# A mixture-of-experts slot loop: GpSimd's scatter moved behind the next slot's power, with four output buffers

## The chip, the cores and the metric

The kernel runs on one core of one Trainium2 chip. A core has five engines that run side by side: TensorE (PE: matmuls and transposes), VectorE (DVE), ScalarE (ACT), GpSimd (POOL) and SyncE (SP), and 16 DMA engines that carry the transfers. The engines wait for each other with semaphores only; each runs its own instructions in order. The metric is the time of one execution on the device, in microseconds, as the median over runs.

## The reference, cut to what matters

Tokens x (2048 rows of 512) first pass a quantized graph layer with an adjacency matrix (2048 x 2048), then a top-2 mixture of 16 experts. The change lies in the second part:

```python
x = x + gnn(layernorm(x), adj, ...)
xn = layernorm(x)
logits = xn @ Wr + br
topk_w, topk_idx = top_k(softmax(logits), 2)        # weights scaled to a sum of 1
h = einsum('nc,ech->neh', xn, W1) + b1
h = gelu(layernorm(h, g1, be1))
y = einsum('neh,eho->neo', h, W2) + b2
out = x + sum over the two chosen experts of topk_w * y
```

All of it is float32. The kernel computes an expert only for the tokens that chose it.

## The kernel before

**Stages.** From 0 to about 220 us the graph layer and the routing run. After them comes the stage of experts, written as slots. A slot is 128 tokens of one expert. The 4096 choices make 39 slots; one of expert 0 is computed early, and slots 0 to 37 form the loop. The last slot of an expert is padded, its spare rows go to rows behind the output. The number of slots is found at run time: `rest` is 17 here, and pair j of the loop is slots 2j and 2j+1, for j from 1 to rest; slots 36 and 37 end it. The experts after the first ones take 1 to 4 slots each; in this input new experts start at slots 5, 7, 10, 13, 16, 18, 19, 21, 23, 24, 28, 30, 32 and 36, and the first three slots (0, 1, 2) alternate between experts 1 and 0, so each counts as a start as well.

**What a slot does.** Rows of normed tokens are gathered from `xn_rows` into `xg` by an indirect DMA of GpSimd (line 747). TensorE transposes them (line 1756), ScalarE and VectorE make a high and a low part (lines 967 and 1392), and TensorE multiplies three times by the weights' high and low parts (lines 1846, 1850, 1854). VectorE takes the statistics of the result (lines 1396 to 1399), GpSimd makes the reciprocal root with a power (line 758, the `power` of this document, output `h_rs`), and VectorE norms (line 1483, `h_hat`). TensorE transposes that (line 1870), ScalarE applies gelu and makes the high part (lines 1021, 1026), VectorE the low one (line 1488), and TensorE multiplies by the second weights (lines 1846 to 1854 again). ScalarE scales the product with the gate into `y_sb` (line 1000), and GpSimd adds these rows to `out` with an accumulating indirect DMA (line 774, the scatter).

**What sets the order.** Everything is ordered by hand, in software pipelining. TensorE's slot s is: transpose h_hat of s (line 1870), transpose the rows of s+3 (line 1756), second layer of s-1, first layer of s+2. GpSimd's iteration s (line 796) is: power of slot s+1, `fetch(s)`, which waits for the gate value of slot s+3 and then gathers the rows of slot s+5, and `give(s - 1)`, which scatters slot s-1. GpSimd runs in order, so while the scatter waits, nothing behind it starts.

**What a scatter waits for** (lines 778 to 783). Two scatters in flight must not add to the same row. Within an expert all rows differ, so only two conditions remain: the scatter of slot s-2 has landed, and, where slot s starts an expert (`start` is 1), that of slot s-1 too. Landings are counted on two semaphores, `scattered[0]` for even and `scattered[1]` for odd slots, 16 for each DMA. Each semaphore begins with 16 from a DMA that fills the spare rows (line 647). The third wait, `y_ok`, is for ScalarE's product. ScalarE in turn waits, ahead of line 1000, until the scatter that used the same half of `y_sb` (slot n-2) has landed.

**Weights.** SyncE loads the weights of an expert's two layers (1 MB each, lines 602 to 609) when those of the expert two before have been split. ScalarE and VectorE split them into high and low parts at each start of an expert (lines 1004 to 1008 and 1460).

**Memory.** `y_sb` holds 2 buffers of 128 x 512, in the space of the support matrix `sup`, which the expert stage no longer needs. Behind `sup` lies the space of the adjacency steps, also free by then.

Of the kernel before, what the change touches and what calls it, by code (L numbers as in the profile page):

```python
# [30 lines left out]
P = 128  # L31
# [154 lines left out]
def gnn_moe_program(nc, x, adj_steps, gnn_w, scalars, wr, br, w1, b1, g1, be1, w2, b2, consts, xn_rows, bias_dram, out):  # L186
    with ExitStack() as ctx:
# [117 lines left out]
        y_sb = place("y_sb", [P, 2, D], F32)  # L305
# [4 lines left out]
        assert where[0] <= end_sup  # L310

# [303 lines left out]
        def _(pool):  # L615
# [31 lines left out]
            for h in range(2):  # L647
                pool.dma_start(out[N + h * P // 2:N + (h + 1) * P // 2, :], k_sb[h * P // 2:(h + 1) * P // 2, 0:D]
                               ).then_inc(scattered[h], 16)
# [122 lines left out]
            def add_rows(at, par):  # L772
                pool.sem_inc(pool_turn, 1)
                pool.indirect_dma_start(  # L774
                    out, bass.IndirectOffsetOnAxis(ap=at, axis=0),
                    y_sb[:, par, :], None, compute_op=ALU.add).then_inc(scattered[par], 16)

            def give(s, start):

                pool.wait_ge(scattered[s % 2], s // 2 * 16 + 16)  # L780
                pool.wait_ge(scattered[1 - s % 2], start * 16 + (s + 1) // 2 * 16)
                pool.wait_ge(y_ok, s + 3)
                add_rows(scat_i[:, s:s + 1], s % 2)
# [9 lines left out]
            give(0, 1)  # L793
            def pool_pair(j):
                earlier, word = load_begins(pool, j - 1), load_begins(pool, j)
                for s in (2 * j, 2 * j + 1):
                    slot_rstd(s + 1, (s + 1) % 2)
                    fetch(s)
                    give(s - 1, (word & 1) if s % 2 else (earlier >> 1))
# [9 lines left out]
            def give_last(back, done, starts):  # L809

                par = (3 - back) % 2
                pool.wait_ge(scattered[par], done)
                pool.wait_ge(scattered[1 - par], starts)
                pool.wait_ge(y_ok, rest * 2 + (4 + back))
                add_rows(idx_s[:, back:back + 1], par)
# [10 lines left out]
        def _(act):  # L826
# [169 lines left out]
            def gated(n, par, landed):  # L996

                act.wait_ge(mm2, n + 1)
                act.wait_ge(scattered[par], landed)
                act.activation(y_sb[:, par, :], y_ps(par), ACT.Copy, scale=gate[:, bass.ds(n + 1, 1)]).then_inc(y_ok, 1)  # L1000
# [33 lines left out]
            def slot(s, par, word, landed, last=False):  # L1034
# [7 lines left out]
                gated(s - 1, 1 - par, landed)  # L1042
# [14 lines left out]
            slot(1, 1, word, 16)  # L1057
            def act_pair(j):
                word = load_plan(act, j)
                for par in range(2):  # L1060
                    slot(j * 2 + par, par, word, j * 16 + 16 * par)
# [9 lines left out]
            for par in range(2):  # L1071
                slot(rest * 2 + (2 + par), par, word, rest * 16 + (16 + 16 * par), last=True)
            gated(rest * 2 + 3, 1, rest * 16 + 32)
# [893 lines left out]
```

## Time and profile before

| | us |
|---|---|
| median of 3 runs | 496.46 |
| lowest and highest run | 492.79, 497.95 |
| profiled execution, its own time | 496.7 |
| its span (first to last instruction) | 494.9 |
| TensorE busy | 456.1 (92%) |
| VectorE busy | 349.9 (71%) |
| ScalarE busy | 306.5 (62%) |
| GpSimd busy | 231.2 (47%) |
| GpSimd, scatter of line 774 (35 of the 38; the last 3 take their indices from `idx_s`) | 64.2 busy, 35.5 idle ahead of it |
| GpSimd, gather of line 747, 40 | 47.3 busy, 57.5 idle ahead of it |
| GpSimd, power of line 758, 38 | 25.1 busy, 31.4 idle ahead of it |
| granted TensorE clock, mean | 0.985 |

Busy time is that in which an engine works on an instruction; for an indirect DMA it is the time in which GpSimd writes its descriptors, and the transfer goes on after it. An idle time stands with what ended it. A row of a timeline has the start, the duration, the engine, the line, the operation, what is written and read, how many instructions were merged, and in brackets the idle time of the engine ahead of it with its releaser. The chain that ended last is followed back from the last instruction, at each step to what released it.

### The profile page before, as it was taken

To read this page: it belongs to the slowest core of one execution; us is meant where nothing else is said; L and a number is where in the kernel's file an instruction comes from. 1 tells how busy PE (TensorE), PEld (TensorE's weight loads), DVE (VectorE), ACT (ScalarE), POOL (GpSimd) and SP (SyncE) were. 2 spreads that over 40 slices of the span, in tenths; PEclk is the share of its full clock that TensorE was granted. 3 is DMA by queue.
4 is the path that set the end of the run, shared out by engine and by line. 5 is a ranking of instruction groups with operands and counts; after the bars stand their busy time and mean duration, and the time that the engine had idled before them with its cause. 6 is when DMAs were issued, how large, how long until landed. Compare 5 with 4: busy or idle time off the path is not lost.

```text
span 494.9 us, 10329 instructions
## 1 busy us (share of the span) xinstructions
PE 456.1 (92%) x2260; PEld 376.2 (76%) x2261; DVE 349.9 (71%) x735; ACT 306.5 (62%) x511; POOL 231.2 (47%) x267
## 2 busy tenths in 40 slices
PE   0799999989999999989899999999899989999990
PEld 0578888877888888867677888888787768888870
DVE  5898863777788877875657786667877777677720
ACT  1667462474544334445787878788888777897550
POOL 4373330332155637553446555554645455356532
PEclk9999999999999999898999999999999999999996
DMA  8621224884655643249849787958699879674543
GB/s 304 262 84 45 86 64 171 299 303 171 221 162 172 214 134 134 84 115 315 260 114 272 186 239 210 263 124 233 210 250 296 248 188 323 149 192 87 86 67 42
DMA packets 33533, 91.30 MB, mean 184 GB/s; under 512 B 6161, under 2 KB 6305, under 8 KB 32993
## 3 DMA queue, kind: packets, MB, share of 16 engines
q1 hardware_dynamic: 19664, 60.60, 36.9%
q0 software_dynamic: 9232, 21.98, 20.9%
q10 hardware_dynamic: 4608, 8.39, 4.6%
q8 instruction: 11, 0.18, 0.1%
q14 instruction: 18, 0.14, 0.1%
HBM read 71.89 MB, written 19.07 MB: 184 GB/s over the span
## 4 chain that ended last, share of the span: by engine, by line
PE 68%; DMA 11%; DVE 6%; issue 5%; ACT 3%; POOL 2%; DVEq 1%; POOLq 1%; ACTq 0%; SPq 0%
PE ps L1595 15%; PE ps L1846 10%; PE ps L1854 9%; PE ps L1850 9%; PE ps L1567 6%; PE ps L1579 6%; DMA out<-y_sb,scat_i 5%; PE ps L1756 3%; PE ps L1870 2%; DMA xg<-xn_rows,tok_i 2%; PE ps L1635 2%; PE ps L1555 1%; DMA xn_rows<-xn 1%; PE ps L1699 1%; DMA gw_raw<-in_gnn_w 1%
## 5 line engine op out<-in xcount | busy, mean ns | idle before, releaser
L774 POOL DMA_INDIRECT out<-y_sb,scat_i x35 | 64.2, 1835 | 35.5 <-DMA out<-y_sb,scat_i 21.9
L1460 DVE TENSOR_TENSOR w_split<-w_raw,w_split x56 | 67.1, 1220 | 12.1 <-issue 9.7
L747 POOL DMA_INDIRECT xg<-xn_rows,tok_i x40 | 47.3, 1183 | 57.5 <-ACT gate L972 49.0
L1021 ACT ACTIVATE g_sb<-ps,be_sb,g_sb 128x128 f32<-128x128 f32 x152 | 57.0, 456 | 16.0 <-PE ps L1870 15.8
L832 ACT ACTIVATE adj_hi<-adj_raw,small 128x1024 fp32r<-128x1024 f32 x32 | 36.8, 1150 | 41.4 <-PE ps L1595 34.5
L1007 ACT ACTIVATE w_split<-w_raw x28 | 53.0, 1912 | 7.8 <-DMA w_raw<-in_w 6.6
L1153 DVE SCALAR_TENSOR_TENSOR adj_lo<-adj_raw,small,adj_hi 128x1024 fp32r<-128x1024 f32 x32 | 40.8, 1275 | 20.6 <-ACT adj_hi L832 20.5
L1595 PE MATMUL ps<-sup,adj_lo 128*128 128x512 f32 x192 | 49.2, 398 | 0.0
L1595 PE MATMUL ps<-sup,adj_hi 128*128 128x512 f32 x192 | 49.2, 398 | 0.0
L1483 DVE TENSOR_SCALAR h_hat<-ps,h_mv,h_rs 128x512 f32<-128x512 f32 x38 | 30.7, 808 | 23.1 <-POOL h_rs L758 23.1
L658 POOL TENSOR_SCALAR rstd<-mv 128x1 f32<-128x1 f32 x15 | 13.7, 914 | 67.6 <-DVE mv L1193 67.5
L1846 PE MATMUL ps<-w_split,gt_hi 128*128 x152 | 44.5, 415 | 0.6 <-ACT gt_hi L1026 0.6
L1854 PE MATMUL ps<-w_split,gt_hi 128*128 x152 | 41.1, 392 | 1.5 <-DVE w_split L1460 1.5
L1488 DVE TENSOR_TENSOR gt_lo<-g_sb,gt_hi 128x512 fp32r<-128x512 f32 x38 | 26.2, 688 | 22.6 <-issue 18.2
L1850 PE MATMUL ps<-w_split,gt_lo 128*128 x152 | 41.0, 392 | 0.1
L1846 PE MATMUL ps<-w_split,xt_hi 128*128 x148 | 40.9, 399 | 0.0
L1595 PEld LDWEIGHTS ps<-sup,adj_lo 128*128 128x128 f32 x192 | 34.9, 188 | 6.9
L1850 PE MATMUL ps<-w_split,xt_lo 128*128 x148 | 40.2, 394 | 0.0
L1595 PEld LDWEIGHTS ps<-sup,adj_hi 128*128 128x128 f32 x192 | 35.0, 188 | 6.8
L758 POOL TENSOR_TENSOR h_rs<-h_rs,k_sb 128x1 f32<-128x1 f32 x38 | 25.1, 662 | 31.4 <-DVE h_rs L1399 31.4
L1854 PE MATMUL ps<-w_split,xt_hi 128*128 x148 | 39.7, 390 | 0.0
L1000 ACT ACTIVATE y_sb<-ps,gate 128x512 f32<-128x512 f32 x38 | 26.1, 687 | 16.6 <-PE ps L1854 15.9
(216 smaller groups left out, 958.0 us busy)
## 6 DMA issues: line engine op xcount, KB each, us to landing
w_raw<-in_w SPq DMA_DIRECT2D x64, 512.0 KB, 6.5
adj_raw<-in_adj_steps SPq DMA_DIRECT2D x32, 512.0 KB, 3.5
out<-x_sb ACTq DMA_DIRECT2D x16, 256.0 KB, 2.9
xn_rows<-xn ACTq DMA_DIRECT2D x16, 256.0 KB, 3.0
bias_rows<-in_b SPq DMA_DIRECT2D x16, 256.0 KB, 3.3
x_sb<-in_x SPq DMA_DIRECT2D x3, 1024.0 KB, 12.3
gw_raw<-in_gnn_w SPq DMA_DIRECT2D x1, 1024.0 KB, 4.9
x_sb<-in_x SPq DMA_DIRECT2D x2, 512.0 KB, 6.8
```

What stands on the lines that cost most here:

```text
L747: return pool.indirect_dma_start(to, None, xn_rows, bass.IndirectOffsetOnAxis(ap=tok_i[:, s:s + 1], axis=0)).then_inc(landed[s % 2], 16)
L774: pool.indirect_dma_start(out, bass.IndirectOffsetOnAxis(ap=at, axis=0), y_sb[:, par, :], None, compute_op=ALU.add).then_inc(scattered[par ...
L832: act.activation(adj_hi[:, par, :], adj_raw[:, par, :], ACT.Copy, scale=small[:, 0:1]).then_inc(adj_hi_ok, 1)
L1007: act.activation(w_parts(n, 0, e + 1), w_raw[:, n, :, :].rearrange("p a n -> p (a n)")[:, at], ACT.Copy).then_inc(split_hi[n], 1)
L1021: ins = act.activation(g_sb[:, par, c * P:(c + 1) * P], ht_ps(par)[:, c * P:(c + 1) * P], ACT.Gelu, scale=g1_sb[:, bass.ds(e * C + c, 1)], ...
L1153: dve.scalar_tensor_tensor(adj_lo[:, par, :], adj_raw[:, par, :], small[:, 0:1], adj_hi[:, par, :].bitcast(F32), ALU.mult, ALU.subtract).t ...
L1460: return dve.tensor_tensor(w_parts(n, 1, e + 1, 2 * h, 2), w_raw[:, n, :, :].rearrange("p a n -> p (a n)")[:, at], w_parts(n, 0, e + 1, 2 ...
L1483: dve.tensor_scalar(h_hat[:, par, :], h_ps(par), h_mv[:, par, 0:1], h_rs[:, par, 0:1], ALU.subtract, ALU.mult).then_inc(h_hat_ok, 1)
L1595: ins = pe.matmul(acc_bank(t), part[:, n % 2, k * P:(k + 1) * P], sup[:, first_k + k, :], start=first_k + k == 0 and not half, stop=first_ ...
L1846: pe.matmul(dst, act_hi[:, par, c * P:(c + 1) * P], w_part(n, 0, e, c), start=False, stop=False, skip_group_check=n == 1)
L1850: pe.matmul(dst, act_lo[:, par, c * P:(c + 1) * P], w_part(n, 0, e, c), start=False, stop=False, skip_group_check=n == 1)
L1854: ins = pe.matmul(dst, act_hi[:, par, c * P:(c + 1) * P], w_part(n, 1, e, c), start=False, stop=c == C - 1, skip_group_check=n == 1)
```

## The change

The order within GpSimd's iteration s becomes: power of slot s+1, scatter of slot s-2, gather of slot s+5. Each slot's scatter so goes out about one slot later than before. Slot 0's scatter moves from ahead of the loop into the first pair. For the last pair (`rest == j`, decided at run time) the scatter of slot 2j is issued behind the pair, so the three last scatters find everything before them issued.

The product lives longer, so it gets four buffers in turn (`y_ring`, by slot modulo 4), and the last three slots have buffers of their own (`y_last`). Both lie in the space of the adjacency steps. ScalarE waits for the landing of the scatter of slot n-4 instead of n-2, and for none in the last three slots. The spare rows are filled by four DMAs of 32 rows instead of two of 64, so each semaphore begins with 32; all counts of landings rise by 16, with ScalarE's in the loop left as they were, which is what moves its wait back by two slots. What each scatter itself waits for stays the same.

```diff
@@ -302,12 +302,16 @@
-        y_sb = place("y_sb", [P, 2, D], F32)
...
+        where[0] = end_sup
+        y_ring = place("y_ring", [P, 4, D], F32)
+        y_last = place("y_last", [P, 3, D], F32)
+        assert where[0] <= w_at
@@ -644,9 +648,9 @@
-            for h in range(2):
-                pool.dma_start(out[N + h * P // 2:N + (h + 1) * P // 2, :], k_sb[h * P // 2:(h + 1) * P // 2, 0:D]
-                               ).then_inc(scattered[h], 16)
+            for h in range(4):
+                pool.dma_start(out[N + h * P // 4:N + (h + 1) * P // 4, :], k_sb[h * P // 4:(h + 1) * P // 4, 0:D]
+                               ).then_inc(scattered[h % 2], 16)
@@ -769,18 +773,18 @@
             def give(s, start):
 
-                pool.wait_ge(scattered[s % 2], s // 2 * 16 + 16)
-                pool.wait_ge(scattered[1 - s % 2], start * 16 + (s + 1) // 2 * 16)
+                pool.wait_ge(scattered[s % 2], s // 2 * 16 + 32)
+                pool.wait_ge(scattered[1 - s % 2], start * 16 + ((s + 1) // 2 * 16 + 16))
                 pool.wait_ge(y_ok, s + 3)
-                add_rows(scat_i[:, s:s + 1], s % 2)
+                add_rows(scat_i[:, s:s + 1], y_ring[:, s % 4, :], s % 2)
@@ -790,13 +794,15 @@
             pool.wait_ge(e_scattered, 16)
-            give(0, 1)
             def pool_pair(j):
-                earlier, word = load_begins(pool, j - 1), load_begins(pool, j)
+                earlier = load_begins(pool, j - 1)
                 for s in (2 * j, 2 * j + 1):
                     slot_rstd(s + 1, (s + 1) % 2)
+                    give(s - 2, (earlier >> (s % 2)) & 1 if j > 1 or s % 2 else 1)
                     fetch(s)
-                    give(s - 1, (word & 1) if s % 2 else (earlier >> 1))
+                if j >= SURE:
+                    with pool.If(rest == j):
+                        give(2 * j, load_begins(pool, j) & 1)
@@ -809,10 +815,10 @@
-                pool.wait_ge(scattered[par], done)
-                pool.wait_ge(scattered[1 - par], starts)
+                pool.wait_ge(scattered[par], done + 16)
+                pool.wait_ge(scattered[1 - par], starts + 16)
                 pool.wait_ge(y_ok, rest * 2 + (4 + back))
-                add_rows(idx_s[:, back:back + 1], par)
+                add_rows(idx_s[:, back:back + 1], y_last[:, back, :], par)
@@ -993,11 +999,12 @@
-            def gated(n, par, landed):
+            def gated(n, par, rows, landed=None):
 
                 act.wait_ge(mm2, n + 1)
-                act.wait_ge(scattered[par], landed)
-                act.activation(y_sb[:, par, :], y_ps(par), ACT.Copy, scale=gate[:, bass.ds(n + 1, 1)]).then_inc(y_ok, 1)
+                if landed is not None:
+                    act.wait_ge(scattered[par], landed)
+                act.activation(rows, y_ps(par), ACT.Copy, scale=gate[:, bass.ds(n + 1, 1)]).then_inc(y_ok, 1)
@@ -1054,11 +1061,12 @@
             def act_pair(j):
                 word = load_plan(act, j)
                 for par in range(2):
-                    slot(j * 2 + par, par, word, j * 16 + 16 * par)
+                    slot(j * 2 + par, par, word, y_ring.rearrange("p a d -> p (a d)")[:, bass.ds(((j * 2 + (par + 3)) & 3) * D, D)],
+                         j * 16 + 16 * par)
```

GpSimd's instructions of one pair in the middle of the loop, before. `TENSOR_TENSOR h_rs` is the power, `DMA xg` the gather, `DMA out` the scatter, `TENSOR_LOAD begins` reads the flags of expert starts into a register; of the two such loads that a pair begins with, the second is the first row here.

```order
L491 TENSOR_LOAD begins
L491 ISA x2
L758 TENSOR_TENSOR h_rs<-h_rs,k_sb 128x1
L747 DMA xg<-xn_rows,tok_i 128x528
L781 ISA
L774 DMA out<-y_sb,scat_i 2176x512
L758 TENSOR_TENSOR h_rs<-h_rs,k_sb 128x1
L747 DMA xg<-xn_rows,tok_i 128x528
L781 REGISTER_ALU
L781 ISA
L774 DMA out<-y_sb,scat_i 2176x512
```

The same pair after the change:

```order
L495 TENSOR_LOAD begins
L495 ISA x2
L762 TENSOR_TENSOR h_rs<-h_rs,k_sb 128x1
L785 REGISTER_ALU
L785 ISA
L778 DMA out<-y_ring,scat_i 2176x512
L751 DMA xg<-xn_rows,tok_i 128x528
L762 TENSOR_TENSOR h_rs<-h_rs,k_sb 128x1
L785 REGISTER_ALU x2
L785 ISA
L778 DMA out<-y_ring,scat_i 2176x512
L751 DMA xg<-xn_rows,tok_i 128x528
```

In both halves of the pair the scatter stood behind the gather, so just ahead of the next half's power, and now it stands between the power and the gather. One load of the flags is gone, and a compare (line 804) with the scatter of slot 2j behind it is new; that part is skipped in all pairs but the last.

Behind the stage's entry the scatter of slot 0 was the last instruction ahead of the first pair. The rows of GpSimd around the first pair's beginning, before:

```order
L758 TENSOR_TENSOR h_rs<-h_rs,k_sb 128x1
L747 DMA xg<-xn_rows,tok_i 128x528
L774 DMA out<-y_sb,scat_i 2176x512
L491 TENSOR_LOAD begins
L491 ISA x2
L491 TENSOR_LOAD begins
L491 ISA x2
L758 TENSOR_TENSOR h_rs<-h_rs,k_sb 128x1
L747 DMA xg<-xn_rows,tok_i 128x528
L781 ISA
L774 DMA out<-y_sb,scat_i 2176x512
L758 TENSOR_TENSOR h_rs<-h_rs,k_sb 128x1
```

and after:

```order
L762 TENSOR_TENSOR h_rs<-h_rs,k_sb 128x1
L751 DMA xg<-xn_rows,tok_i 128x528
L495 TENSOR_LOAD begins
L495 ISA x2
L762 TENSOR_TENSOR h_rs<-h_rs,k_sb 128x1
L778 DMA out<-y_ring,scat_i 2176x512
L751 DMA xg<-xn_rows,tok_i 128x528
L762 TENSOR_TENSOR h_rs<-h_rs,k_sb 128x1
L785 REGISTER_ALU x2
L785 ISA
L778 DMA out<-y_ring,scat_i 2176x512
L751 DMA xg<-xn_rows,tok_i 128x528
```

The first power of the pair (slot 3) had the scatter of slot 0 ahead of it and has nothing of the kind now, and slot 0's and slot 1's scatters follow the powers of slots 3 and 4.

## Rows read from the trace of the kernel before

**Rows 1.** The page, section 4: shares of the chain that ended last.

```profile
PE 68%; DMA 11%; DVE 6%; issue 5%; ACT 3%; POOL 2%; DVEq 1%; POOLq 1%; ACTq 0%; SPq 0%
```

**Rows 2.** The chain that ended last: start us, us, what.

```profile
363.57 8.91 DMA out<-y_sb,scat_i
```

**Rows 3.** Windows: us, PE, PEld, DVE, ACT, POOL busy (x), PEclk, DMA share, GB/s.

```profile
241.40:268.00 26.60, 25.90 (x129) 21.12 (x128) 16.86 (x30) 19.81 (x38) 14.55 (x13) 1.00 0.69 173
...
341.00:407.00 66.00, 61.16 (x301) 49.48 (x300) 51.22 (x76) 53.50 (x93) 32.86 (x28) 1.00 0.81 234
407.00:473.00 66.00, 66.00 (x333) 55.37 (x334) 45.79 (x76) 49.78 (x95) 36.51 (x32) 1.00 0.67 166
```

**Rows 4.** Timeline of TensorE: start us, us, engine line op, [idle before <-releaser].

```profile
255.06 0.66 PE L1870 MATMUL ps<-k_sb,h_hat 128*128 128x128 f32 x4 [0.26 <-DVE h_hat L1483]
...
262.31 0.66 PE L1870 MATMUL ps<-k_sb,h_hat 128*128 128x128 f32 x4 [0.44 <-DVE h_hat L1483]
...
301.89 0.60 PE L1870 MATMUL ps<-k_sb,h_hat 128*128 128x128 f32 x4
...
308.47 0.60 PE L1870 MATMUL ps<-k_sb,h_hat 128*128 128x128 f32 x4
...
349.41 0.65 PE L1870 MATMUL ps<-k_sb,h_hat 128*128 128x128 f32 x4 [1.30 <-issue]
...
377.26 0.65 PE L1870 MATMUL ps<-k_sb,h_hat 128*128 128x128 f32 x4 [1.15 <-DVE h_hat L1483]
...
384.35 0.60 PE L1756 MATMUL ps<-k_sb,xg 128*128 128x128 f32 x4
...
402.44 1.20 PE L1854 MATMUL ps<-w_split,gt_hi 128*128 x4 [1.47 <-DVE w_split L1460]
```

**Rows 5.** Timeline of GpSimd, an undisturbed slot.

```profile
303.39 0.57 POOL L758 TENSOR_TENSOR h_rs<-h_rs,k_sb 128x1 f32<-128x1 f32 x1 [0.94 <-DVE h_rs L1399]
305.69 1.01 POOL L747 DMA_INDIRECT xg<-xn_rows,tok_i  x1 [1.73 <-ACT gate L972]
307.40 2.13 POOL L774 DMA_INDIRECT out<-y_sb,scat_i  x1 [0.70 <-issue]
```

**Rows 6.** Waits, 240 to 496 us: us in total, times, longest us.

```profile
POOL out L774 <- DMA out<-y_sb,scat_i: 21.9, 8, 5.8
```

**Rows 7.** Timeline of GpSimd, the stage's beginning.

```profile
251.96 1.60 POOL L774 DMA_INDIRECT out<-y_sb,scat_i  x1 [5.75 <-DMA out<-y_sb,scat_i]
253.01 1.14 POOL L758 TENSOR_TENSOR h_rs<-h_rs,k_sb 128x1 f32<-128x1 f32 x1
```

**Rows 8.** Timeline of VectorE around late powers.

```profile
249.28 0.15 DVE L1399 TENSOR_SCALAR h_rs<-h_mv 128x1 f32<-128x1 f32 x1
254.19 0.81 DVE L1483 TENSOR_SCALAR h_hat<-ps,h_mv,h_rs 128x512 f32<-128x512 f32 x1 [4.76 <-POOL h_rs L758]
...
374.12 0.15 DVE L1399 TENSOR_SCALAR h_rs<-h_mv 128x1 f32<-128x1 f32 x1
...
396.44 0.81 DVE L1483 TENSOR_SCALAR h_hat<-ps,h_mv,h_rs 128x512 f32<-128x512 f32 x1 [1.69 <-POOL h_rs L758]
```

**Rows 9.** Timeline of GpSimd, slots 21 to 24.

```profile
373.33 1.58 POOL L774 DMA_INDIRECT out<-y_sb,scat_i  x1 [2.47 <-DMA out<-y_sb,scat_i]
374.39 1.12 POOL L758 TENSOR_TENSOR h_rs<-h_rs,k_sb 128x1 f32<-128x1 f32 x1
375.70 1.01 POOL L747 DMA_INDIRECT xg<-xn_rows,tok_i  x1 [0.19 <-issue]
...
395.29 1.12 POOL L758 TENSOR_TENSOR h_rs<-h_rs,k_sb 128x1 f32<-128x1 f32 x1
```

**Rows 10.** Timeline of ScalarE, a split that waits for weights.

```profile
387.00 1.92 ACT L1007 ACTIVATE w_split<-w_raw  x1 [3.89 <-DMA w_raw<-in_w]
```

**Rows 11.** Line 774, the scatter: from issue to landing.

```profile
DMA to landing us min/median/max: 4.8/8.5/9.7
```

**Rows 12.** Line 747, the gather: from issue to landing.

```profile
DMA to landing us min/median/max: 3.3/4.4/8.0
```

More of the change, by code:

```diff
@@ L770, in fetch, with add_rows @@
                 gather(s + 5)
-            def add_rows(at, par):
+            def add_rows(at, rows, par):
                 pool.sem_inc(pool_turn, 1)
@@ L775, in add_rows @@
                     out, bass.IndirectOffsetOnAxis(ap=at, axis=0),
-                    y_sb[:, par, :], None, compute_op=ALU.add).then_inc(scattered[par], 16)
+                    rows, None, compute_op=ALU.add).then_inc(scattered[par], 16)
             def give(s, start):
-                pool.wait_ge(scattered[s % 2], s // 2 * 16 + 16)
-                pool.wait_ge(scattered[1 - s % 2], start * 16 + (s + 1) // 2 * 16)
+                pool.wait_ge(scattered[s % 2], s // 2 * 16 + 32)
+                pool.wait_ge(scattered[1 - s % 2], start * 16 + ((s + 1) // 2 * 16 + 16))
                 pool.wait_ge(y_ok, s + 3)
-                add_rows(scat_i[:, s:s + 1], s % 2)
+                add_rows(scat_i[:, s:s + 1], y_ring[:, s % 4, :], s % 2)
             early_scatter()
@@ L1032, in slot_seed, with slot @@
                 act.activation(y_ps(par), bias_rows2[:, bass.ds((e & 3) * D, D)], ACT.Copy).then_inc(y_seeded, 1)
-            def slot(s, par, word, landed, last=False):
+            def slot(s, par, word, rows, landed=None, last=False):
                 e_s, e_a = expert_in(word, par), expert_in(word, par + 2)
@@ L1041, in slot @@
                     slot_gate(s + 3, 1 - par, expert_in(word, par + 3))
-                gated(s - 1, 1 - par, landed)
+                gated(s - 1, 1 - par, rows, landed)
                 if not last:
@@ L1056, in _ @@
             split_next(1, expert_in(word, 0), starts_in(word, 0))
-            slot(1, 1, word, 16)
+            slot(1, 1, word, y_ring[:, 0, :])
             def act_pair(j):
@@ L1071, in _ @@
             for par in range(2):
-                slot(rest * 2 + (2 + par), par, word, rest * 16 + (16 + 16 * par), last=True)
-            gated(rest * 2 + 3, 1, rest * 16 + 32)
+                slot(rest * 2 + (2 + par), par, word, y_last[:, par, :], last=True)
+            gated(rest * 2 + 3, 1, y_last[:, 2, :])
             for par in range(2):
@@ L1076, in _ @@
             for i in range(2):
-                act.wait_ge(scattered[i], rest * 16 + 48)
+                act.wait_ge(scattered[i], rest * 16 + 64)
             act.sem_inc(all_landed, 1)
```

## The prediction

> **What bounds the kernel now.** I read the chain that ended last first, then the stages in windows, then TensorE's timeline slot by slot, then GpSimd's. The chain is 68% TensorE, but 11% of the span on it is DMA [rows 1], and the scatter of line 774 is its largest part. One piece of the chain is the 8.91 us in which slot 18's scatter, issued at 363.57, lands [rows 2]. The windows show where TensorE is not full. From 241.40 to 268.00 it is busy 25.90 of 26.60 us, from 341 to 407 it is busy 61.16 of 66.00, and from 407 to 473 all 66.00 [rows 3]. The granted clock is 1.00 in all three. So the expert stage runs at TensorE's own pace except in two places, with 0.70 and 4.84 us of idle time.
>
> The pace is one slot per 6.58 us: slot 11's hidden transpose starts at 301.89 and slot 12's at 308.47 [rows 4]. I write S for the time at which a slot's hidden transpose starts. A slot can gain only where its distance from the one before exceeds 6.58. These are slot 4 (7.05, from slot 3 at 248.01), slot 5 (7.25), slot 18 (349.41, 8.04 after slot 17), slot 22 (377.26, 7.94 after slot 21), slot 24 (7.43) and slot 26 (8.87, with the wait at 402.44 inside it); all other excesses are 0.1 or less. The sum of all excesses from slot 2 to slot 36 is 7.7 us, the ceiling of the whole change. Slot 18's part, 1.46 us, is "issue", a wait for nothing in the profile, which I leave out. That leaves 6.2.
>
> **What happens on GpSimd.** In an undisturbed slot (S = 301.89) the power starts at S+1.50, the gather at S+3.80 and the scatter at S+5.51, for 2.13 us [rows 5]. The scatter is the last thing before the next power, which comes at S+8.08. If the scatter waits for its predecessor to land, the power behind it is late. Line 774 waits for a landing 8 times, 21.9 us in all, at most 5.8 [rows 6]. At slot 4 this reaches TensorE. The scatter at 251.96 waited 5.75 us, the power behind it ended at 254.15 [rows 7], though VectorE had asked for it at 249.28+0.15. VectorE waited 4.76 us with h_hat [rows 8], and TensorE started its transpose at 255.06 [rows 4].
>
> **The change, part by part.**
>
> (1) The order in a slot becomes power, scatter of slot s-2, gather. The product that the scatter takes has long been ready (it was made in the slot before, at about S-2), so the scatter waits for no ScalarE and can start at about S+1.50+0.57+0.3 = S+2.4. The gather follows: before, GpSimd stood idle there for 1.73 us, waiting for the gate value [rows 5]. The scatter takes 1.6 to 2.6 us, so the gather starts at S+4.2 to S+5.3 instead of S+3.8.
>
> Gain at slots 4 and 5: both excesses (0.47 and 0.67) come from the late power, the second because VectorE is then late with the splits and statistics of the next slot. With the power in front, it starts at about S(3)+1.5 = 249.5 and not 253.01. I take both in full and the 0.1 behind them: -1.2.
>
> Gain at slot 22: the power starts at 374.39 and takes 1.12 us instead of 0.57, since the scatter issued at 373.33 still runs [rows 9]. VectorE's request was ready at 374.27 [rows 8]. Without the scatter it would end at about 375.0 instead of 375.5: 0.5 us at most. The rest of this excess is older than GpSimd's part. ScalarE and VectorE were themselves late with weight splits, and the next split waits 3.89 us for a weight transfer that lands at 387.0 [rows 10]; the gain at 22 is likely absorbed there. I take 0.2, with 0 and 0.5 as bounds, and nothing for slot 24.
>
> Gain at slot 26: the power at 395.29 takes 1.12 us behind a scatter [rows 9], and VectorE waits 1.69 us for it instead of the 0.6 or so of a power alone [rows 8]. From there the chain runs through VectorE's sequencer and a split to the matmul at 402.44. I take 0.8, with 0 and 2.3 as bounds.
>
> (2) The ring of four. ScalarE waits for the landing of slot n-4 instead of n-2. This wait was seen once, 0.7 us, with ScalarE idle right behind it for a weight transfer: nothing. The ring is also what makes (1) legal, as the scatter now reads the product one slot later. Its register address costs ScalarE two sequencer instructions a slot, in slots where it has idle time.
>
> (3) Two more small DMAs at the start, about 1 us of GpSimd each by the gather's row [rows 5]. They lie in the support phase and feed nothing but a semaphore and, behind them, casts first used in the adjacency windows: nothing. Were that cover gone, 2 us.
>
> (4) The end. The scatter of slot 2*rest still goes out one slot early, behind an If, and the last three keep their places and their waits; the buffers of their own remove waits of ScalarE that had already ended. Nothing. Two loads of "begins" per pair become one, and a compare is added: nothing.
>
> (5) What is pushed back is the gather, and this is the cost. The gather issued in slot s is used by the row transpose of slot s+2, 0.43 us behind its hidden transpose, so at S+13.6; it had 9.8 us. Gathers take 3.3 to 8.0 us, median 4.4 [rows 12]. The tightest one now is issued at 375.70, takes the 8.0 and lands at 383.7; the transpose starts at 384.35 [rows 4, 9]. It has 0.6 us to spare. In the changed kernel its scatter (slot 19, a start of an expert behind another) must first see slot 18 land, at about 374.3, if that one is issued at 365.4 and takes its 8.9 us again [rows 2]. Then the scatter goes at 375.3, the gather at 377.2, and it lands 1.5 us later than before, or 0.9 us too late for TensorE. In the other slots with an expert start the scatter waits 0 to 3 us and the gather lands 0.7 before to 0.7 behind its use. I take +0.9, with 0 and +7 as bounds (below).
>
> Something speaks for a higher price. The gather of 8.0 us was issued only 2.4 us behind a scatter [rows 9], the quiet gather at 305.69 nearly 5 us behind one, and the median gather takes 4.4. The Trainium skill (DMA: Bandwidth & Descriptors, Two DMAs through the same engine are not ordered) states that within one queue of an engine descriptors start in order. By that rule a gather right behind a scatter cannot land much ahead of it: in two or three more slots with weight transfers it would come in too late, and the sum would be about 2 us higher; without it the 0.9 stands. By it, the one row agrees, and it is part of what rival (A) below would look like.
>
> **Sum.** -1.2 - 0.2 - 0.8 + 0.9 = -1.3 us on the profiled execution's 496.7 us (its span of 494.9 and 1.8 around it): 495.4. That execution lies 0.2 above the median of the three runs, 496.46, so I name 495.2.
>
> **Rivals.**
>
> (A) The gather becomes the wait. A scatter that lands 8.5 us (median) to 9.7 us behind its issue [rows 11], one slot of 6.58 before, makes the next expert's first scatter wait 1.9 to 3.1 us, plus some 0.9 from landing to issue. The gather then starts as late as S+2.4+4.0+2.1+0.3 = S+8.8, and with a latency of 4.4 to 8.0 lands at S+13.2 to S+16.8, against S+13.6: up to 3.2 us late. This would show as TensorE waiting at line 1756 on the DMA of xg. With all 8 waits ending in a gather 0.9 us late, 7.2 us are lost and 2.2 gained: 501.7, or 501.5 against the median. With three such (2.7 lost) the result is 497.0, so from the third on the change loses. Against it: each stall of TensorE also gives the scatters time. It is the case of the other side. Chance 0.2, of which 0.1 over 1%.
>
> (B) The dense stretch clears. The chain runs from 355.0 to 373.3 through the landings of two scatters. If these, and not the weights, set VectorE's lateness, slots 22, 24 and 26 return their 1.36 + 0.85 + 2.29 = 4.5 us; with the 1.2 and no late gather that is 491.0, or 490.8 against the median. For it: the chain itself [rows 2]. Against it: the splits wait for weight transfers at 387.0 [rows 10], and VectorE's request at slot 22 was only 0.1 us ahead of the power. Chance 0.17.
>
> (C) Nothing moves. The weight transfers hold the dense stretch, the first cluster's 1.2 us is eaten by one late gather, and the change does not do what it says because the scatter still stands ahead of the next power and can run into it. GpSimd's room ahead of the next power grows from 0.4 us (scatter's end to S+8.08) to between 1.8 and 2.8 (gather's end at S+5.2 to S+6.3), so a longer wait still reaches the power. That gives 496.5. Chance 0.13.
>
> The forecast itself, 493.5 to 496.2, has 0.5.
>
> **From the cases to the numbers.** About 1% (5 us) is what a measurement of this kernel can tell from no change; its own three runs span 492.79 to 497.95. Faster by over 1% means under 491.5: most of (B), 0.13. Slower by over 1% means over 501.4: half of (A), 0.1. Same: 0.77. The range goes from 490.5, just beyond (B), to 499.5, which holds the milder half of (A), with 10% left out above and a few per cent below.
>
> **What would show it.** Right: powers of slots 4 and 5 at S+1.5 of the slot before; TensorE's busy time in 241 to 268 full; no power of over 0.6 us that starts inside a scatter; no wait of h_hat for the power above 0.7 us. Step (5): a wait at line 1756 for xg around slot 23, of under 2 us, and gather starts between S+4.2 and S+5.3 in slots without an expert start. Wrong: waits at line 1756 in four slots or more (A); slots 22 to 26 all 6.6 apart (B); a ScalarE wait for scattered, or the last three scatters later against TensorE's end.

## The result and the profile after

The change makes the kernel slower: median 497.28 us of 20 runs (494.42 to 500.36), against 493.67 us for the kernel before in the same session (20 runs, 491.14 to 497.95). The ratio is 1.0062, 95% interval 1.0041 to 1.0082. A second comparison gave 1.0086 (1.0058 to 1.0114). The forecast was 1.3 us faster, so it is wrong in sign, though the time lies in its range and within 1% of the kernel before. The forecast's base also moved: 496.46 us was the median of three runs, and the median of 20 is 2.8 us lower. Ratios leave out the executions of a kernel that were over 1.5% longer than its fastest, so they can differ from the quotient of two medians.

The profiled execution of after took 496.24 us, with a span of 494.4. That is no longer than the one of before, but before's began its slots late: slot 2's hidden transpose starts at 241.40 there and at 238.52 here. So the two are compared from slot 2's transpose to slot 36's, and from there to the end.

| us | before | before, 2nd profile | after | after, 2nd profile |
|---|---|---|---|---|
| slot 2 to slot 36 (34 slots; 223.7 at 6.58 each) | 231.4 | 231.2 | 233.1 | 232.7 |
| slot 36 to the end | 22.1 | 22.0 | 22.8 | 23.0 |
| TensorE's waits for gathered rows, slot 2 to 36 | none | 0.2 | 5.0 | 3.7 |

On average the slots cost 1.6 us more and the end 0.8. The medians differ by 3.6 and 3.5 us; about 1 us of it is in none of these four profiles.

The page of after, section 4, the chain that ended last by engine (before: [rows 1]); and from section 5 GpSimd's three groups: line, engine, operation, count, then busy us, mean ns, and idle us ahead with the main releaser.

```profile
PE 54%; DMA 15%; issue 12%; POOL 6%; DVE 5%; ACT 3%; ACTq 1%; POOLq 1%; SPq 0%; DVEq 0%
...
L778 POOL DMA_INDIRECT out<-y_ring,scat_i x35 | 65.1, 1860 | 24.0 <-DMA out<-y_ring,scat_i 12.7
...
L751 POOL DMA_INDIRECT xg<-xn_rows,tok_i x40 | 48.0, 1200 | 24.1 <-ACT gate L978 11.0
L762 POOL TENSOR_TENSOR h_rs<-h_rs,k_sb 128x1 f32<-128x1 f32 x38 | 22.1, 582 | 74.5 <-DVE h_rs L1407 74.3
```

The power is no longer held up: 582 ns mean, and its idle time ends with VectorE's statistics. The scatter's idle time fell from 35.5 to 24.0 us. But the gather's idle time fell too, from 57.5 to 24.1 us. Most of it had been a wait for the gate value, so it was reserve: the gather could not start earlier, but what stood ahead of it could take longer without moving it. The waits from slot 2 to slot 36 of after, in us in total, times, longest:

```profile
DVE h_hat L1491 <- POOL h_rs L762: 16.5, 23, 1.5
POOL out L778 <- DMA out<-y_ring,scat_i: 12.7, 12, 4.3
PEld ps L1764 <- DMA xg<-xn_rows,tok_i: 6.6, 7, 1.8
PE ps L1764 <- DMA xg<-xn_rows,tok_i: 5.0, 6, 1.5
```

The first two lines are what the change aims at: against [rows 6] the scatter's waits fell from 21.9 to 12.7 us, and VectorE's longest wait for a power from 4.76 [rows 8] to 1.5. One more wait, 2.8 us ahead of slot 1's scatter at 250.03, stands in the profile as one for ScalarE's product, but that product was written at 242.70; slot 0's scatter, which it needs, landed at 249.14. The last two lines are new. TensorE's timeline has four of the six:

```profile
259.69 0.66 PE L1764 MATMUL ps<-k_sb,xg 128*128 128x128 f32 x4 [0.80 <-DMA xg<-xn_rows,tok_i]
300.30 0.66 PE L1764 MATMUL ps<-k_sb,xg 128*128 128x128 f32 x4 [0.34 <-DMA xg<-xn_rows,tok_i]
341.43 0.66 PE L1764 MATMUL ps<-k_sb,xg 128*128 128x128 f32 x4 [0.98 <-DMA xg<-xn_rows,tok_i]
384.04 0.66 PE L1764 MATMUL ps<-k_sb,xg 128*128 128x128 f32 x4 [1.52 <-DMA xg<-xn_rows,tok_i]
```

The others are at 398.51 (0.94 us) and 412.48 (0.39 us). The rows waited for are those of slots 8, 14, 20, 26, 28 and 30 (TensorE is in slots 5, 11, 17, 23, 25 and 27). Each of these gathers stands behind the scatter of the first slot of an expert (slots 1, 7, 13, 19, 21, 23). One of them, slot 20's, on GpSimd's timeline of after:

```profile
329.51 0.57 POOL L762 TENSOR_TENSOR h_rs<-h_rs,k_sb 128x1 f32<-128x1 f32 x1 [4.27 <-DVE h_rs L1407]
330.53 2.33 POOL L778 DMA_INDIRECT out<-y_ring,scat_i  x1 [0.46 <-issue]
333.17 1.54 POOL L751 DMA_INDIRECT xg<-xn_rows,tok_i  x1 [0.30 <-issue]
```

and the same place in before, where the gather came straight behind the power:

```profile
331.26 0.57 POOL L758 TENSOR_TENSOR h_rs<-h_rs,k_sb 128x1 f32<-128x1 f32 x1 [1.49 <-DVE h_rs L1399]
332.02 1.99 POOL L747 DMA_INDIRECT xg<-xn_rows,tok_i  x1 [0.19 <-issue]
334.32 2.12 POOL L774 DMA_INDIRECT out<-y_sb,scat_i  x1 [0.31 <-issue]
```

Slot 15 starts at 326.60 in after and at 328.21 in before. The power comes 2.9 us behind that start in after (3.05 in before), not 1.5, because it waits for VectorE's statistics. No landing is waited for here. The gather starts at S+6.57, against S+3.81 in before, and its rows land 8.2 us later, at 341.38, just as TensorE begins at 341.43.

The line that times the gather from issue to landing in after (before: [rows 12]), then the scatter's (before: [rows 11]):

```profile
DMA to landing us min/median/max: 3.3/5.7/8.3
```

```profile
DMA to landing us min/median/max: 4.7/5.6/10.2
```

The gather's median rose from 4.4 to 5.7 us and the scatter's fell from 8.5 to 5.6. Both steps are too large: [rows 11] holds the landings of the even slots' scatters alone, since two records of the odd ones are missing in that profile. In the second profiles, which have all landings, the gather's median is 4.9 in before and 5.1 in after, and the scatter's 6.8 and 5.7.

### The profile page after: what moved, and what is told of

Same layout as the page of the kernel before. It is cut to its first block, busy times and chain, and to the rows that moved or that the text cites. A ratio compares the mean times of both kernels' runs of the same rounds, so it can differ in the third digit from the quotient of the medians.

```text
span 494.4 us, 10394 instructions
## 1 busy us (share of the span) xinstructions
PE 456.0 (92%) x2260; PEld 375.8 (76%) x2261; DVE 350.7 (71%) x735; ACT 306.0 (62%) x511; POOL 232.3 (47%) x269
## 4 chain that ended last, share of the span: by engine, by line
PE 54%; DMA 15%; issue 12%; POOL 6%; DVE 5%; ACT 3%; ACTq 1%; POOLq 1%; SPq 0%; DVEq 0%
PE ps L1603 15%; DMA xg<-xn_rows,tok_i 7%; PE ps L1575 6%; PE ps L1587 6%; PE ps L1854 6%; PE ps L1862 5%; PE ps L1858 5%; DMA out<-y_ring,scat_i 4%; POOL out L778 2%; POOL xg L751 2%; PE ps L1643 2%; PE ps L1764 2%; PE ps L1563 1%; DMA adj_raw<-in_adj_steps 1%; PE ps L1878 1%
## 5 line engine op out<-in xcount | busy, mean ns | idle before, releaser
L778 POOL DMA_INDIRECT out<-y_ring,scat_i x35 | 65.1, 1860 | 24.0 <-DMA out<-y_ring,scat_i 12.7
L751 POOL DMA_INDIRECT xg<-xn_rows,tok_i x40 | 48.0, 1200 | 24.1 <-ACT gate L978 11.0
L762 POOL TENSOR_TENSOR h_rs<-h_rs,k_sb 128x1 f32<-128x1 f32 x38 | 22.1, 582 | 74.5 <-DVE h_rs L1407 74.3
L1404 DVE BATCH_NORM_STATS2 h_stats<-ps 128x6 f32<-128x512 f32 x38 | 26.3, 693 | 15.6 <-PE ps L1862 15.4
```

What stands on the lines that cost most here:

```text
L751: return pool.indirect_dma_start(to, None, xn_rows, bass.IndirectOffsetOnAxis(ap=tok_i[:, s:s + 1], axis=0)).then_inc(landed[s % 2], 16)
L778: pool.indirect_dma_start(out, bass.IndirectOffsetOnAxis(ap=at, axis=0), rows, None, compute_op=ALU.add).then_inc(scattered[par], 16)
```

## The experiments

**Theory 1**: the order on GpSimd makes the loss, since the gather now stands behind power and scatter and comes too late in some slots; the ring costs nothing. **Rivals**: the loss is the ring's or its place in memory; or the late powers remain; or the slots' excesses belong to the weights and the waits for rows only show beside them. All ratios are against the kernel before on the same chip.

| run | median, us | ratio (95%) | slot 2 to 36 | to the end | waits for rows |
|---|---|---|---|---|---|
| ring_only | 493.32 | 1.0007 (0.9970 to 1.0044) | 232.0 | 22.2 | 0 |
| order_only | 497.01 | 1.0066 (1.0037 to 1.0095) | 234.6 | 22.7 | 5.0 |
| gather_first | 501.35 | 1.0143 (1.0094 to 1.0191) | 235.6 | 22.6 | 0 |
| no_scatter | 490.55 | 0.9914 (0.9881 to 0.9946) | 226.9 | 20.5 | 0 |
| pad_scatter | 488.19 | 0.9884 (0.9868 to 0.9901) | 226.3 | 20.5 | 0 |
| after_xg | 491.75 | 0.9942 (0.9906 to 0.9979) | 230.1 | 22.2 | 0 |
| after_xg_again | 491.65 | 0.9981 (0.9948 to 1.0015) | 229.7 | 22.0 | 0 |
| after_xg_third | 492.32 | 0.9971 (0.9949 to 0.9993) | 229.7 | 22.2 | 0 |
| before_xg | 493.28 | 0.9981 (0.9955 to 1.0007) | 229.4 | 21.9 | 0 |
| before_xg_again | 492.54 | 0.9983 (0.9945 to 1.0021) | 233.6 | 21.9 | 0 |

### The parts apart: ring alone, order alone

The ring, the last slots' own buffers and the four fills, with the old order of scatters (against after; the scatter behind the last pair goes too):

```diff
+            give(0, 1)
...
-                earlier = load_begins(pool, j - 1)
+                earlier, word = load_begins(pool, j - 1), load_begins(pool, j)
-                    give(s - 2, (earlier >> (s % 2)) & 1 if j > 1 or s % 2 else 1)
                     fetch(s)
...
+                    give(s - 1, (word & 1) if s % 2 else (earlier >> 1))
```

> The four buffers, the three of the last slots, the four fill DMAs and the counts, but GpSimd's old order: power, gather, scatter of slot s-1. Theory 1 (the loss is the gather that starts behind the scatter): ratio to before 0.998 to 1.001, TensorE waits for xg 0 times in the slots, and the late powers at slots 4, 5, 22 and 26 are there again. Rival (the loss lies in the other parts: register addresses on ScalarE, the fill DMAs): ratio 1.003 to 1.008.

Ratio 1.0007: these parts cost nothing that can be measured, as steps (2) and (3) of the prediction had it. The new order with two buffers for y (against after):

```diff
-        y_ring = place("y_ring", [P, 4, D], F32)
+        y_ring = place("y_ring", [P, 2, D], F32)
...
-                add_rows(scat_i[:, s:s + 1], y_ring[:, s % 4, :], s % 2)
+                add_rows(scat_i[:, s:s + 1], y_ring[:, s % 2, :], s % 2)
...
-                         j * 16 + 16 * par)
+                         j * 16 + (16 + 16 * par))
```

> The new order on GpSimd with y in two buffers instead of four (the last slots keep three of their own): ScalarE writes y of slot n when the scatter of slot n - 2 has landed. Theory 1 (the order alone makes the loss): that scatter is issued 2 to 5 us into slot n and y of slot n is written 4.3 us into the next slot, 6 to 9 us later, and scatters land 4.8 to 10.2 us after their start: ScalarE waits in a few slots, 1 to 5 us in all, and the time is that of after or up to 2 us more, ratio to before 1.004 to 1.012. Rival (the larger ring or its place in memory makes the loss): ratio 0.998 to 1.002, as with the ring alone.

Ratio 1.0066, the loss of after, so the loss is the order's. TensorE waits for rows here too, 5.0 us in six waits. ScalarE's waits were mis-sized: 19.4 us where 1 to 5 were expected.

```profile
ACT y_ring L1007 <- DMA out<-y_ring,scat_i: 19.4, 8, 3.7
```

Its slots took 1.5 us more than after's first profile, but its median is not above after's (497.01 against 497.28 and 497.77), so nothing shows that the two extra buffers earn anything. In after the same view puts 4.9 us of ScalarE's waits on landings, but each of those products was started 0.36 us behind the end of TensorE's last matmul for it, as in the slots with no such entry: they are waits for TensorE.

### The second profiles

> The kernel after once more, for a second profile. Theory 1: TensorE waits at least 2 us in all for gathered rows in the loop, in slots whose gather stands behind a scatter of an odd slot, ratio to before 1.003 to 1.009. Rival (the waits of the first profile were chance): under 1 us, ratio the same.

3.7 us of waits for rows, in slots 9, 17, 23, 25 and 29 (after's first profile: 5, 11, 17, 23, 25 and 27): the mechanism is there again, in partly other slots.

> The kernel before once more, for a second profile of the slot loop. Theory 1 (the first profiles told the truth on the loop): from slot 2's hidden transpose to slot 36's some 231 us (231.4 in the first profile; 233.1 and 232.7 in the two of after), at least one power held up by a scatter that waits for a landing, no wait of TensorE for gathered rows over 0.5 us, and 22.1 us from slot 36 to the end (22.8 and 23.0 in after). Rival (the loop's times differ by chance): 232.5 us or more, or waits for rows.

231.2 us, as expected. But the excesses are elsewhere. GpSimd's timeline in this second profile of before has the late power of [rows 7] again:

```profile
248.76 1.60 POOL L774 DMA_INDIRECT out<-y_sb,scat_i  x1 [4.71 <-DMA out<-y_sb,scat_i]
249.82 1.14 POOL L758 TENSOR_TENSOR h_rs<-h_rs,k_sb 128x1 f32<-128x1 f32 x1
```

A landing that was waited for 1 us less was enough: from slot 3's transpose to slot 6's it is 0.23 us over the pace, against 1.25 in the first profile. So the 1.2 us that the prediction put there is the size of one execution.

### The gather ahead of the scatter

Power, gather, scatter of slot s-2 (against after):

```diff
-                    give(s - 2, (earlier >> (s % 2)) & 1 if j > 1 or s % 2 else 1)
                     fetch(s)
+                    give(s - 2, (earlier >> (s % 2)) & 1 if j > 1 or s % 2 else 1)
```

> The changed kernel with two lines exchanged: power, gather, scatter of slot s-2. The scatter needs no wait for ScalarE's product, so it can start about 0.6 us sooner than in the kernel before, and the gather starts as before. Theory 1: no wait of TensorE for xg, powers less late than before, ratio to before 0.994 to 1.000. Rival (it is the scatter that comes one slot later, or the ring, that costs): ratio 1.003 to 1.008 like the changed kernel.

The waits for rows are gone, and the kernel is the slowest of all, where 0.994 to 1.000 was expected and the rival had 1.008 at most. GpSimd's timeline, and VectorE's at the same place:

```profile
275.95 1.02 POOL L751 DMA_INDIRECT xg<-xn_rows,tok_i  x1 [0.19 <-issue]
282.37 1.57 POOL L778 DMA_INDIRECT out<-y_ring,scat_i  x1 [5.40 <-DMA out<-y_ring,scat_i]
283.43 1.13 POOL L762 TENSOR_TENSOR h_rs<-h_rs,k_sb 128x1 f32<-128x1 f32 x1
```

```profile
279.77 0.15 DVE L1407 TENSOR_SCALAR h_rs<-h_mv 128x1 f32<-128x1 f32 x1
284.60 0.81 DVE L1491 TENSOR_SCALAR h_hat<-ps,h_mv,h_rs 128x512 f32<-128x512 f32 x1 [4.67 <-POOL h_rs L762]
```

The scatter stands last ahead of the next power again. It waits 5.40 us for its predecessor to land, and the power that VectorE asked for at 279.92 runs at 283.43; slots 8 and 9 then took 6.95 and 9.06 us, since VectorE was late with the next splits and statistics as well. This is the late power of before, [rows 7, 8], with longer waits (28.8 us in 7 waits for landings against 21.9 in 8). The one-slot delay of the scatter does not protect the power: each scatter still has only the one ahead of it to wait for, issued about a slot earlier. What protects the power is the place, and that place is paid for by the gather.

### Time on GpSimd, or the scatter's packets?

The scatters of slots 0 to 33 and ScalarE's waits for their buffers are left out, so the output lacks these slots; in the second run a fill of an unused buffer stands in the scatter's place:

```diff
-                    give(s - 2, (earlier >> (s % 2)) & 1 if j > 1 or s % 2 else 1)
+                    pool.wait_ge(y_ok, s + 1)
...
+                    pool.memset(pad_sb[:, :], 0.0).then_inc(pad_ok, 1)    # the second run only
                     fetch(s)
```

> The kernel after, without the scatters of slots 0 to 33 (they, their waits for landings and the multiplier engine's wait for their buffers are left out, so these slots' results are not added to the output; the scatters behind the loop stay). GpSimd then does power and gather and nothing between. Theory 1 (the gather, standing behind power and scatter, became late; the scatter costs nothing else): no wait of TensorE for gathered rows within the loop, no scatter in front of a power, so of the 9.4 us that the slots 2 to 36 take over 6.58 us each in the profile of after, the 5.0 us of waits for rows go, and what weights cost (slots 17, 23 to 26) stays: 3 to 7 us less than after, ratio to before 0.988 to 0.998. Rival (the slots' lateness is that of the weights and VectorE's splits, the rows' lateness only shows beside it): the waits for rows vanish but the slots stay at 8 to 10 us over, ratio 1.000 to 1.006.

> As the run without scatters, but GpSimd fills a buffer that nobody reads (128 x 2048, whose like took 1.81 us elsewhere in the kernel) where the scatter stood, behind the power and ahead of the gather: the time on GpSimd stays about that of the scatter (1.9 us mean), its packets and its waits for landings are gone. Theory 1a (the gather is late because it is issued late): TensorE still waits 2 to 5 us in all for rows in the slots where VectorE's splits hold the power back, the time is within 2 us of after's (ratio to before 1.001 to 1.008). Theory 1b (it is late because its packets stand behind the scatter's in one queue, or behind a scatter that waits for a landing): the gather's latencies in these slots fall from 7.4 to 8.3 us to 4 to 7 us, the waits are under 1 us in all, and the time is that of the run without scatters to 1 us.

Both lose the waits for rows. In the run with the fill the place of slot 20's gather reads (its slot 15 starts at 322.56, so the gather at S+5.55):

```profile
325.61 0.56 POOL L765 TENSOR_TENSOR h_rs<-h_rs,k_sb 128x1 f32<-128x1 f32 x1 [4.65 <-DVE h_rs L1416]
326.13 1.80 POOL L807 MEMSET pad_sb<- 128x2048 f32 x1
328.11 0.99 POOL L754 DMA_INDIRECT xg<-xn_rows,tok_i  x1 [0.17 <-issue]
...
DMA to landing us min/median/max: 3.3/4.0/7.1
```

The six gathers that were late, by their start behind S of the slot in which they are issued, and from start to landing, all in us:

| rows of slot | before | after | fill, no scatter |
|---|---|---|---|
| 8 | 6.3, 3.8 | 6.9, 7.6 | 4.0, 4.4 |
| 14 | 3.8, 6.8 | 6.4, 7.7 | 5.2, 4.0 |
| 20 | 3.8, 7.2 | 6.6, 8.2 | 5.6, 4.3 |
| 26 | 6.4, 8.0 | 8.9, 7.4 | 6.0, 7.0 |
| 28 | 8.4, 5.6 | 8.8, 7.7 | 6.5, 6.7 |
| 30 | 6.9, 7.7 | 7.2, 8.3 | 7.3, 5.9 |
| mean | 5.9, 6.5 | 7.5, 7.8 | 5.8, 5.4 |

From before to after they start 1.5 us later and take 1.3 us longer. With the fill they start 1.7 us earlier than in after, since the scatter takes up to 2.7 us and sometimes waits, and they land 2.4 us quicker. So 1.8 us of time on GpSimd alone (theory 1a of the expectation) make nobody late. But the run does not hold the start of these gathers fixed: they start as early as in before (5.8 against 5.9), so how much of the lateness is the later start and how much the longer transfer is not separated.

The six places were picked because they were late in this profile of after, which makes the growth look large. In the second profiles the means of the same six are 5.6 and 6.7 in before and 7.3 and 7.5 in after: 1.7 us later, and 0.8 longer.

Why they take longer, the landings suggest. In both profiles of before and both of after, 34 gathers each from slot 7's rows on, not one of the 136 landed ahead of the scatter issued before it; the nearest was 0.6 us behind. In each profile of after 14 of 34 landed within 1 us of it, in those of before 10 and 8. The gather is issued 2.2 us behind a scatter in after and 4.5 in before (means), so by this reading it inherits more of what is left of the scatter's latency. The Trainium skill (DMA: Bandwidth & Descriptors, Two DMAs through the same engine are not ordered) says that within one queue of an engine descriptors start in order but are pipelined, and it promises no order of completion; in these traces the landings were in order too. Where the gather goes ahead of the scatter, the scatter has the longer latency: 4.9 and 6.8 us in before's second profile (medians). What the runs do not separate is the order in the queue from the scatter's traffic as such: without it the DMA engines are also less busy, 0.53 of the time instead of 0.77.

The slots take 226.3 to 226.9 us without scatters, 2.6 to 3.2 above the pace. So the scatter, by whatever way, costs the loop some 4.7 us in before and 6.3 in after. That the run with the fill is 2.4 us faster in the median than the one without does not come from these slots; in the profile without the fill TensorE waited 3.4 us ahead of slot 2 for one gather (1.5 with it), and no run shows whether it did so each time.

### Room for the gather

Four buffers for gathered rows, the gather of slot s+6 in iteration s, a slot earlier; TensorE's loop is unrolled twice, so the buffer's number is fixed in the code. The same in before is the control. The core of the edit:

```diff
...
-        xg = place("xg", [P, 2, ROW], F32)
+        xg = place("xg", [P, 4, ROW], F32)
...
-                pool.wait_ge(gate_ok, s + 4)
-                gather(s + 5)
+                pool.wait_ge(gate_ok, s + 3)
+                gather(s + 6)
```

> The changed kernel with a ring of four for xg and each gather issued one slot earlier (slot s+6 in iteration s), with TensorE's loop written out for two pairs, since its transposes need fixed addresses. A gather then has 6.58 us more. Theory 1: the 5.0 us of TensorE's waits for xg vanish and the powers stay punctual: ratio to before 0.988 to 0.996. Rival (the late gathers only cover another limit, the weight transfers and splits, which then shows at the same slots): ratio 1.001 to 1.006, with waits for w_split or gt_hi of several us in place of those for xg.

> The kernel before with the same ring of four for xg, gathers one slot earlier and the same loop of TensorE: the control for the run above. The kernel before has no wait for xg in its slots, so theory 1: ratio 0.998 to 1.003, late powers as before. If the loop written out costs something by itself (code), it shows here: over 1.003.

> The kernel after with gathered rows in four buffers and the gather a slot earlier, once more. Theory 1: no wait for rows, loop 230 us, ratio to before 0.992 to 0.997, and 2 us below its control with the old order (the gain that steps 1 to 3 of the prediction name, 2.2 us, is there once the gather cannot be late). Rival (the new order brings nothing even then): within 0.5 us of its control.

> The control: the kernel before with the same four buffers and the earlier gather. Theory 1: late powers stay, ratio to before 0.996 to 1.001, 2 us above the run with the new order. Rival: within 0.5 us of it.

> The new order with gathered rows in four buffers and the gather a slot earlier, a third time, since its first two comparisons gave 0.9942 and 0.9981. If its gain is real: ratio 0.994 to 0.998 with an interval below 1, no wait of TensorE for gathered rows, 229.5 to 231 us from slot 2 to slot 36. If the first comparison was luck: ratio 0.998 to 1.001.

With the new order the kernel goes from 1.006 and 1.009 to 0.994, 0.998 and 0.997: some 5 us below after, and below the kernel before in all three (in two of them with an interval under 1; 0.998 is outside the 0.992 to 0.997 expected for it). The gather's line in the first of these profiles shows why. In after it sat idle 11.0 us for the gate value, here 0.6, and from the slots on nobody waits for its rows (the one wait that is left is ahead of slot 2):

```profile
  issue: 11.2, 38
  DVE tok_i L1449: 3.7, 1
  ACT gate L984: 0.6, 2
who waited for it (us, times):
  PEld ps L1771: 1.4, 1
  PE ps L1771: 1.0, 1
```

These buffers do two things. They take the late rows out of the loop, and they take 1.8 us out of slot 1, just ahead of slot 2 (5.6 to 3.8 us long), which the control gains too. So the fair comparison is with the control, before_xg: from 3.6 us slower than its counterpart the new order goes to 1.5 and 0.9 us faster in the medians (2.2 was expected). The late gather, then, is the cause of the loss in the slots; the end's 0.8 us has a cause of its own (below). That the sign turns is not shown, as the intervals overlap.

The same profiles price the late rows. From slot 2 to slot 36 after takes 232.9 us on average, and 229.8 with the four buffers, so by this estimate the late rows cost some 3 us and not the 5.0 that TensorE waited. The third rival holds for a part: slot 23 is 8.43 and 8.26 us long in after, where it waited 1.5 and 1.3 us for rows, and 8.28, 7.79 and 8.48 with the buffers, where it waits for nobody's rows but for VectorE at its end:

```profile
385.79 0.66 PE L1885 MATMUL ps<-k_sb,h_hat 128*128 128x128 f32 x4 [1.54 <-DVE h_hat L1497]
```

Slots 17 (8.07 against 8.2 to 8.3) and 25 (7.90 against 7.6 to 7.7) are much the same. What the late rows lengthen for good are the others: slots 5 and 6 together, 11 and 27, over the pace by 1.59, 0.67 and 0.75 us in after's first profile.

The control keeps the late powers, in its second profile more of them than the kernel before has, and its loop took 229.4 us in one profile and 233.6 in the other:

```profile
POOL out L778 <- DMA out<-y_sb,scat_i: 35.5, 9, 6.3
DVE h_hat L1491 <- POOL h_rs L762: 23.5, 23, 4.1
```

## Why the prediction was wrong

**What held.** The pace of 6.58 us, the place of the late powers, and their cure: from slot 3's transpose to slot 5's there are 6.58 us each again, and from slot 21's to slot 22's too (7.94 before), and no wait of VectorE for a power exceeds 1.5 us. The ring and the fills cost nothing (ring_only). The mechanism of the cost, a wait at the rows' transpose, is the one that step (5) and rival (A) describe.

**Step (5) failed, by its size.** It took +0.9 us, for one late gather. The runs show six late gathers and some 3 us (232.9 us in after's slots against 229.8 with the late rows removed). TensorE's waits add up to 5.0 us, but three of the six fell into slots 17, 23 and 25, which are as long without them: the wait at 341.43 lies in a slot that takes 8.07 us in after and 8.04 in before. Two terms of the step were wrong:

- The gather's start. The prediction had S+4.2 to S+5.3 unless a landing is waited for, from the power at S+1.5. That is an undisturbed slot. Behind a start of an expert VectorE first makes two weight splits (rows below), the power comes at S+2.9, the scatter's descriptors take 2.33 us, and the gather starts at S+6.57 with no landing waited for. Of the six only slot 8's and slot 26's gathers stood behind a scatter that waited. The late power stood in the trace of before (331.26, S+3.05), but the prediction took its terms from one quiet slot.
- Its latency. The prediction kept the old ones. In these six places they grew from 6.5 to 7.8 us in the first profiles and from 6.7 to 7.5 in the second. The prediction named a rule by which they might grow, priced it at 2 us and left it out of the sum. Its sum with them, 497.2, lies close to the measured 497.28, but by chance: it starts from 496.46, and the kernel before measures 493.67. Against the base it would have been 0.7 us slower, where 3.6 was measured.

VectorE's timeline of after, the two splits, then the statistics that the power at 329.51 waits for:

```profile
325.33 2.36 DVE L1468 TENSOR_TENSOR w_split<-w_raw,w_split  x2 [0.25 <-issue]
...
329.27 0.15 DVE L1407 TENSOR_SCALAR h_rs<-h_mv 128x1 f32<-128x1 f32 x1
```

**Step (1) was nearly right in its sum, partly by luck.** It took -2.2 us. With the late rows removed the slots take 229.8 us against 231.3 in before, a gain of 1.4 by the unrounded times. So the slots add up: -1.4 and some +3 give the +1.6 of the table. The parts are uneven. Slot 25 (the prediction's slot 26) went from 8.87 and 8.60 to 7.6 to 7.7 us, 1.1 where 0.8 was summed. Slots 3 to 5, which carried 1.2, are over the pace by 1.25 in one profile of before and 0.23 in the other, and by 0.04 to 0.50 with the buffers. And slot 21's excess of 1.36 did not go: it moved to slots 22 and 23, and the three together take 22.0 and 21.2 us in before, 22.6 and 22.1 in after, and 21.8 to 22.1 with the buffers. The prediction took most of that gain as absorbed there, and it was.

**Step (4), the end, failed by 0.8 us.** At the exit of the loop TensorE's sequencer reads the next plan word twice. These are the reads from 469 us on in after, then in before (min/median/max ns):

```profile
L492 PEldq TENSOR_LOAD <-plan x2: 299/638/978, 469.9 to 471.4; - x2
```

```profile
L488 PEldq TENSOR_LOAD <-plan x2: 305/307/309, 471.0 to 471.8; - x2
```

One read took 0.98 us instead of 0.31, in after's second profile 0.94 and with two buffers 0.96, while both profiles of before and ring_only have 0.31 there. TensorE stood idle 0.69 us right behind it:

```profile
472.89 1.18 PE L1854 MATMUL ps<-w_split,gt_hi 128*128 x4 [0.69 <-ACT ps L1039]
```

The row names ScalarE's seed as the releaser, but TensorE's sequencer reached the matmul only at 472.52, S+0.91, and at 472.90, S+0.12, in before. That a slow read makes the longer end is the reading of these rows; no run changed it alone. With four buffers for rows one of the two reads is slow as well (0.88 to 0.93 us), but the sequencer comes to them 0.6 us earlier (S-2.27 against S-1.66), and the end is 22.0 to 22.2 us. And gather_first has an end of 22.6 us with both reads at 0.3, so a longer end has other causes too. Why the read is slow stays open, as does the 1 us of the medians that no profile shows.

**The rivals.** (A) is what happened, in its mild form: waits in six slots, where the prediction's own sign for it was four or more, and a loss, at a fifth of the chance. Its line "from the third on the change loses" fits. Its price of 0.9 us per wait is the mean idle time (5.0 us in six waits), but not what they cost, some 3 us in all. (B) did not happen: slots 23 and 25 took 8.43 and 7.90 us.

## What to carry to other kernels

On an engine that runs in order, a step is moved into somebody's reserve. Read the reserve of what is pushed back in its worst slots (here the gather's start and landing behind each start of an expert), not in a quiet one, and count the queue position of its transfer as well as its issue. Size a gain that hangs on one wait for a landing by two profiles: a scatter's wait of 5.75 us cost 1.25 us in one, one of 4.71 cost 0.23 in the other. And do not read a wait as a cost: slot 23 lost 1.5 us to late rows in one run and about as much to VectorE in another, where the rows were early.

## What was unexpected of the hardware

- GpSimd's two indirect transfers landed in the order of their issue: none of 136 gathers landed ahead of the scatter issued before it, and 28 of the 68 in after's two profiles landed 0.6 to 1.0 us behind it.
- A sequencer's read of a word of a table takes 0.30 us, but 0.6 to 0.98 us now and then. In after TensorE's sequencer had three such over 0.6 us (at 263.41, 304.02 and 469.95). Within the loop it is hidden; at the loop's exit it is not.
- A transpose that waited for its rows makes its slot longer than the idle time shows: 1.12 us for a wait of 0.80 and 0.67 for 0.34 in after, 0.77 for 0.42 in its second profile and 1.60 for 1.25 in order_only, so 0.32 to 0.35 us more each time. No run shows why.
